# Row-wise attention scores: their causal mask from TensorE to VectorE and GpSimd

## The reference

```python
xn = layernorm(x)
q, k, v = (split_heads(xn @ W.T) for W in (Wq, Wk, Wv))
scores = einsum('bhqd,bhkd->bhqk', q, k) / sqrt(32)
scores = where(tril(ones((S, S))), scores, finfo.min)      # causal, S = 1024
attn = einsum('bhqk,bhkd->bhqd', softmax(scores), v)
gate = silu((xn @ fp8(gate_w)) * gate_scale)               # 512 -> 1536
up = (xn @ fp8(up_w)) * up_scale
ffn = ((gate * up) @ fp8(down_w)) * down_scale             # 1536 -> 512
out = x + merge_heads(attn) @ Wo.T + ffn
```

## Time and profile before

| | |
|---|---|
| median of 3 runs | 1274.52 us (1270.1 to 1280.29) |
| the profiled execution | 1273.23 us |
| its span, first to last instruction | 1271.4 us |
| mean granted TensorE clock | 0.993 |
| PE, DVE, ACT, POOL busy | 96%, 81%, 71%, 69% |

### The profile page before, as it was taken

How to read it: one execution, slowest core, us unless ns; L and a number is a source line. 1 busy time by engine, 2 the same in 40 slices (tenths; PEclk the granted TensorE clock), 3 DMA queues, 4 the chain that set the end, 5 groups by cost and what they waited for, 6 DMA issues and landing times.

```text
span 1271.4 us, 32677 instructions
## 1 busy us (share of the span) xinstructions
PE 1225.1 (96%) x11851; PEld 827.8 (65%) x11852; DVE 1031.0 (81%) x2587; ACT 908.6 (71%) x1555; POOL 875.1 (69%) x1033
## 2 busy tenths in 40 slices
PE   4999998979999999999999999999999999999988
PEld 3444443438677767677777777777777677777763
DVE  8877776768788888888888898888888888888862
ACT  4433433439788878887878898888888887878880
POOL 1333323227777777888888888888888888888882
PEclk9999999989999999999999999999999999999999
DMA  8799989776747485656667676757685766667555
GB/s 268 226 244 258 260 239 237 203 212 142 145 97 160 105 145 114 151 113 147 131 142 156 129 151 129 155 105 157 117 169 118 161 117 145 131 140 154 116 118 126
DMA packets 422319, 201.32 MB, mean 158 GB/s; under 512 B 327056, under 2 KB 390544, under 8 KB 421648
## 3 DMA queue, kind: packets, MB, share of 16 engines
q1 hardware_dynamic: 409312, 179.32, 64.1%
q10 hardware_dynamic: 12848, 19.93, 5.2%
HBM read 76.03 MB, written 44.30 MB: 95 GB/s over the span
## 4 chain that ended last, share of the span: by engine, by line
PE 65%; DMA 3%; ACT 3%; POOL 2%; issue 2%; DVE 2%; SPq 1%; ACTq 0%
PE bank L1653 22%; PE bank L1667 12%; PE bank L1631 10%; PE pair L241 5%; PE pair L1593 5%; PE bank L1675 4%; PE pair L1607 3%; PE pair L1675 2%; DMA p_t<-row 1%; POOL row L1338 1%; PE bank L1690 1%; DMA a_rows<-a_rows 1%; ACT probs L1390 1%; PE bank L294 1%; ACT row L1414 1%
## 5 line engine op out<-in xcount | busy, mean ns | idle before, releaser
L1400 ACT ACTIVATE p<-pair,s_exp 128x512 f32<-128x512 f32 (+1 forms) x384 | 243.5, 634 | 151.2 <-PE pair L1593 144.7
L1338 POOL TENSOR_TENSOR row<-row 128x896 f16<-128x896 f32 (+1 forms) x128 | 256.8, 2010 | 25.5 <-ACT row L1414 25.4
L1171 POOL TENSOR_TENSOR probs<-p,probs 128x512 f16<-128x512 f32 x192 | 221.1, 1158 | 6.8 <-ACT probs L1390 6.6
L1390 ACT CAST probs<-p 128x512 f16<-128x512 f32 (+1 forms) x384 | 215.1, 560 | 7.6 <-POOL p L1332 7.5
L1653 PE MATMUL bank<-shared,wg 128*128 128x256 f16 x1536 | 200.0, 273 | 0.7 <-DVE fu L1531 0.5
L1653 PE MATMUL bank<-shared,wu 128*128 128x256 f16 x1536 | 199.2, 273 | 0.0
L1667 PE MATMUL bank<-wd,fuse 128*128 128x512 f16 x768 | 193.1, 378 | 0.8 <-DVE ff_out L1517 0.8
L1332 POOL TENSOR_SCALAR_AFFINE_SELECT p<-p 128x128 f32<-128x128 f32 (+1 forms) x256 | 109.0, 428 | 103.0 <-ACT p L1400 100.8
L1536 DVE TENSOR_REDUCE row_top<-pair 128x1 f32<-128x896 f32 (+1 forms) x128 | 147.5, 1152 | 25.7 <-PE pair L1611 24.4
L1653 PEld LDWEIGHTS bank<-shared,wg 128*128 128x128 f16 x1536 | 144.3, 98 | 33.6 <-DMA shared<-xn_parts 1.3
L1653 PEld LDWEIGHTS bank<-shared,wu 128*128 128x128 f16 x1536 | 142.2, 98 | 19.5
(11 more groups left out here) (166 smaller groups left out, 2112.3 us busy)
## 6 DMA issues: line engine op xcount, KB each, us to landing
q_st<-q_parts SPq DMA_DIRECT2D x192, 64.0 KB, 2.3
k_st<-k_parts SPq DMA_DIRECT2D x192, 64.0 KB, 1.9
v_parts<-res SPq DMA_DIRECT2D x8, 1056.0 KB, 6.3
v_sb<-v_parts SPq DMA_DIRECT2D x64, 132.0 KB, 2.2
xn_parts<-x_t SPq DMA_DIRECT2D x16, 512.0 KB, 6.6
shared<-xn_parts SPq DMA_DIRECT2D x16, 512.0 KB, 4.7
res<-in_L_attn_x SPq DMA_DIRECT2D x16, 512.0 KB, 4.0
out<-shared SPq DMA_DIRECT2D x32, 256.0 KB, 2.5
```

The source lines that it names most:

```text
L1171: ops.tensor_tensor(probs[n % 2][:, LO, at], p32[e % RING][:, 0:UNIT_WIDTH[u]], probs[n % 2][:, HI, at], ALU.subtract).then_inc(signal, 1)
L1338: nc.gpsimd.tensor_tensor(row16[r][:, w:2 * w], row32[r][:, :], row16[r][:, 0:w], ALU.subtract).then_inc(row_lo, 1)
L1390: nc.scalar.copy(probs[n % 2][:, HI, u * 512:u * 512 + w], p32[e % RING][:, 0:w]).then_inc(p_hi, 1)
L1400: nc.scalar.activation(p32[e % RING][:, 0:w], st_bank[u % 2][:, 0:w], ACT.Exp, scale=s_exp[:, :]).then_inc(exp_done, 1)
```

## The change

The third product of a row tile goes, with its two bf16 tiles. DVE now takes the maximum over the columns ahead of the diagonal block, and then with a second instruction the maximum over the diagonal block plus the mask, starting from the first. The diagonal block's exponentials are therefore unmasked in `row32`, and POOL zeroes their masked half (`cut_row`). ACT's cast waits for POOL's select instead of the exponential. The casts move by one step (6 to 7, 12 to 13), and so do the low parts (8 to 9, 14 to 15).

```diff
--- before.py
+++ after.py
@@ -133,8 +133,9 @@
 ROW_SCORES_STEP = {2: (0,), 6: (1,)}
 ROW_MAX_STEP = {3: (0,), 6: (1,)}
 ROW_EXP_STEP = {4: (0,), 10: (1,)}
-ROW_HIGH_STEP = {6: (0,), 12: (1,)}
-ROW_LOW_STEP = {8: (0,), 14: (1,)}
+ROW_CUT_STEP = {4: (0,), 10: (1,)}
+ROW_HIGH_STEP = {7: (0,), 13: (1,)}
+ROW_LOW_STEP = {9: (0,), 15: (1,)}
 M_STEP = {8: (0, 1), 10: (2,), 11: (3,), 12: (4,), 14: (5,), 16: (6, 7)}
 MAX_STEP = {8: (0, 1), 10: (2,), 12: (3, 4), 13: (5,), 16: (6, 7)}
 MAX_HIGH_STEP = {1: (0,)}
@@ -1068,8 +1069,6 @@
         p_t = sb("p_t", [P, PT_SIZE], F16)
         row_top = sb("row_top", [P, 2], F32)
         row_bias = sb("row_bias", [P, 2], F32)
-        mask_bf = sb("mask_bf", [P, P], mybir.dt.bfloat16)
-        ident_bf = sb("ident_bf", [P, P], mybir.dt.bfloat16)
         rsum = sb("rsum", [P, QB // 2], F32)
         attn = sb("attn", [P, 2, QB, D], F32)
         a_rows = sb("a_rows", [P, 4 * D], F16)
@@ -1108,7 +1107,8 @@
         p_hi = sem("p_hi")
         p_lo_dve = sem("p_lo_dve")
         p_lo_pool = sem("p_lo_pool")
-        bf_set = sem("bf_set")
+        row_open = sem("row_open")
+        row_cut = sem("row_cut")
         row_mm = sem("row_mm")
         row_red = sem("row_red")
         row_bias_set = sem("row_bias_set")
@@ -1301,8 +1301,6 @@
             pool.sem_inc(res_done, 1)
             nc.gpsimd.memset(k_st[3][3 * DK:3 * DK + 2, :], MSCALE).then_inc(ones_set, 1)
             pool.wait_ge(ones_set, 1)
-            nc.gpsimd.tensor_copy(mask_bf[:, :], rows.mask[:, 512 - P:512]).then_inc(bf_set, 1)
-            nc.gpsimd.tensor_copy(ident_bf[:, :], ident[:, :]).then_inc(bf_set, 1)
 
             def add_down(i, t):
 
@@ -1332,6 +1330,13 @@
                 nc.gpsimd.affine_select(out=at, in_=at, compare_op=ALU.is_ge, fill=0.0, base=0,
                                         pattern=[[0, blocks], [1, P]], channel_multiplier=-1).then_inc(diag_done, 1)
 
+            def cut_row(r, n):
+
+                pool.wait_ge(row_exp, 2 * n + r + 1)
+                at = row32[r][:, row_width(r) - P:row_width(r)]
+                nc.gpsimd.affine_select(out=at, in_=at, compare_op=ALU.is_ge, fill=0.0, base=0, pattern=[[-1, P]],
+                                        channel_multiplier=1).then_inc(row_cut, 1)
+
             def low_of_row(r, n):
                 pool.wait_ge(row_hi, 2 * n + r + 1)
                 w = row_width(r)
@@ -1342,6 +1347,8 @@
                 n, k = HEADS_PER_IT * it + s, s * U + u
                 for unit, head in of_head(SELECT_STEP, n, u):
                     select(unit, head)
+                for r, head in of_head(ROW_CUT_STEP, n, u):
+                    cut_row(r, head)
                 for unit, head in of_head(LOW_POOL_STEP, n, u):
                     take_low(pool, nc.gpsimd, POOL_LOW, unit, head, p_lo_pool)
                 for r, head in of_head(ROW_LOW_STEP, n, u):
@@ -1408,7 +1415,7 @@
                                      bias=row_bias[:, r:r + 1], scale=s_exp[:, :]).then_inc(row_exp, 1)
 
             def high_of_row(r, n):
-                act.wait_ge(row_exp, 2 * n + r + 1)
+                act.wait_ge(row_cut, 2 * n + r + 1)
 
                 wait(act, row_turned[r], 16 * n)
                 nc.scalar.copy(row16[r][:, 0:row_width(r)], row32[r][:, :]).then_inc(row_hi, 1)
@@ -1533,8 +1540,12 @@
 
             def maximum_of_row(r, n):
                 dve.wait_ge(row_mm, 2 * n + r + 1)
-                nc.vector.tensor_reduce(row_top[:, r:r + 1], row_bank[r][:, 0:row_width(r)], AX.X, ALU.max
-                                        ).then_inc(row_red, 1)
+                w, top = row_width(r), row_top[:, r:r + 1]
+                nc.vector.tensor_reduce(top, row_bank[r][:, 0:w - P], AX.X, ALU.max).then_inc(row_open, 1)
+                dve.wait_ge(row_open, 2 * n + r + 1)
+                nc.vector.tensor_tensor_reduce(
+                    out=rows.junk[r][:, 0:P], in0=row_bank[r][:, w - P:w], in1=rows.mask[:, 512 - P:512], scale=1.0,
+                    scalar=top, op0=ALU.add, op1=ALU.max, accum_out=top).then_inc(row_red, 1)
                 dve.wait_ge(row_red, 2 * n + r + 1)
                 nc.vector.tensor_scalar(row_bias[:, r:r + 1], row_top[:, r:r + 1], s_neg[:, 0:1], None, ALU.mult
                                         ).then_inc(row_bias_set, 1)
@@ -1604,12 +1615,9 @@
                     pe.wait_ge(exp_done, NE * n + 3)
                 part, i, w = slice(0, 3 * DK), ROWS[r], row_width(r)
                 for at, size in ((0, 512), (512, w - 512)):
-                    nc.tensor.matmul(row_bank[r][:, at:at + size], q_st[s][part, i * P:(i + 1) * P],
-                                     k_st[s][part, at:at + size], start=True, stop=at == 0)
-                if n == r == 0:
-                    pe.wait_ge(bf_set, 2)
-                nc.tensor.matmul(row_bank[r][:, w - P:w], ident_bf[:, :], mask_bf[:, :], start=False,
-                                 stop=True).then_inc(row_mm, 1)
+                    mm = nc.tensor.matmul(row_bank[r][:, at:at + size], q_st[s][part, i * P:(i + 1) * P],
+                                          k_st[s][part, at:at + size], start=True, stop=True)
+                mm.then_inc(row_mm, 1)
 
             def probabilities(n, i, j, part):
 
```

## The result

The changed kernel took 1326.65 us, median of four runs (1324.98 to 1329.09), against 1276.12 us of the kernel before: 1.0407 times as long, 95% interval 1.0364 to 1.0449. Its profiled execution has a span of 1324.1 us at a mean granted clock of 0.991, against 1271.4 at 0.993; by an estimate from these, a clock lower by 0.2% is worth under 3 of the 52.7 us.

What follows compares the result with a forecast made beforehand. TensorE (PE, 96% busy) was taken to bound the kernel, with the cut making it wait for POOL's chain: 1273 + 42 (iterations 4 to 15) + 6 (iterations 0 to 3) = 1321 us, range 1284 to 1355.

Steps and rivals of the forecast that it cites:

- the likeliest case: POOL's late selects delay ACT's row-1 cast and stall PE at full size: from the cheap end to 1355 us, 55%.
- The chain: Row 1's select waits behind row 0's low part on POOL, delaying ACT's cast and tanh, DVE's fu, PE's gate.
- the three named: Heads s = 2, 3 and 1 of each four-head iteration: PE stalls 2.45 (2.0), 1.1 (0.6), 0.8 (0.6) us.
- the wrong wait: In head s = 1, PE stalls 0.8 (0.6) us at gate 5 through the late cast and its tanh.
- 3.8 us less 0.3 of gain per iteration: PE stalls of 3.8 us per four-head iteration, less product gain: 3.5 x 12 iterations (4 to 15) = 42 us.
- the cheap end: POOL's selects at 0.29 us instead of 0.40: stalls of 3.2 us per iteration instead of 4.35.
- the rule: VectorE and GpSimd lock each other out of shared SBUF ports; by it the new selects would be cheap throughout.
- 1312 us: Whole-kernel time with selects at the cheap end throughout: 1273 + 2.9 x 12 + 4, against 1330 at the dear end.
- At most 7.4 us: PE's gain from dropping 128 mask products at 0.058 us each, 0.6% of the time.
- cost nothing more: DVE's 0.45 us stalls at PE's third maxima unit, heads 2 and 3, lie ahead of larger stalls there.
- the rival: Only DVE bites: PE's third maxima unit waits, +0.45 in heads 2 and 3, +0.2 in head 1; 1284 us, 12%.
- The hidden-work rival: POOL's and ACT's waits are absorbed and TensorE's 7.4 us come through: 1266 us, 10%.

Runs made afterwards that it cites:

- pool_only: The changed kernel with the mask products kept on PE and DVE's single maximum kept, so POOL's selects and the casts' waits stand alone: 1327.66 us, 1.0444.
- cut1_early: The changed kernel with row 1's select issued in step 9 instead of 10, ahead of row 0's low part in POOL's list: 1295.88 us, 1.0191.
- pe_dve_only: The changed kernel without POOL's selects, steps as before: no mask products, maximum in two steps, masked half of the exponentials left unzeroed: 1281.36 us, 1.0077.
- no_mask: The kernel before without the 128 mask products and nothing in their place, masked half of the row-wise scores left as it is: 1269.7 us, 0.9986.
- one_pass: The kernel before without mask products; one DVE instruction adds a wide mask in place in PSUM and takes the row maximum, no selects: 1271.87 us, 1.0002.
- placed: The whole change, row 0's select behind m_neg and m_part, row 1's ahead of row 0's low part only where s = 2, low parts at old steps: 1288.6 us, 1.0134.

## Why the prediction was right

The time (1321 us forecast, 1326.65 measured) is inside the range, and it is the likeliest case, not a rival, that happened. By its own steps:

*The chain.* Select behind row 0's low part, cast of row 1, tanh, `fu`, PE's gate: each link is in the waits, and `pool_only` shows that POOL's part is enough by itself. The longer heads are the three named, and head s = 0 has no stall. For s = 2 and s = 3 `cut1_early` shows the chain, as they get 1.34 and 0.71 us shorter when the select comes early. For s = 1 it shows that the prediction had the wrong wait: its 0.96 us stay when the stall at gate 5 goes, and come from POOL's own lateness by ACT's cast of `probs`. It is luck that 0.96 is near the 0.8 (0.6) of the forecast.

*Its size.* 3.8 us less 0.3 of gain per iteration was forecast, 3.82 measured; for the iterations without `a_rows` 1.5, measured 1.8. By head the forecast of the stalls was 2.45 (2.0), 1.1 (0.6) and 0.8 (0.6) us for s = 2, 3 and 1; the heads are 1.80, 1.17 and 0.96 longer, products' gain included. The cast in s = 2 is 2.6 us late, which is the cheap end (2.65). So the choice of 3.8 between the ends came out for a partly wrong reason: the selects are at the cheap end throughout,

```profile
L1337 POOL TENSOR_SCALAR_AFFINE_SELECT row<-row x128: 283/292/311, 282.3 to 1279.6; 128x128 f32<-128x128 f32 x128
```

as the rule had it that the prediction cites from "SBUF — State Buffer" of the Trainium skill, while the time that I worked out from that, 1312 us, was 15 short. The prices of s = 3 and s = 1 are larger than the cheap end gave. The idle times ahead of the cast, 1.98, 1.25 and 0.87 us in s = 2, 3 and 1, are shorter than the 2.5 to 3, 2 and 1 to 1.5 announced, because ACT itself comes later to the cast: in s = 2 it had waited 0.41 us for PE's scores ahead of the exponential before it, and waits 0.91 now.

*PE's gain.* "At most 7.4 us" holds as a bound, and is far too high as a value: 2 us. In the sum this hid, since it counted only 0.3 us an iteration; the changed kernel has 0.19 (63.25 us against 63.44 in `pool_only`). The 0.06 us per product is its time on one chain; without the products, an iteration of the kernel before is 0.31 us shorter instead of 0.46, and the whole run gains less still.

*DVE.* That its stalls "cost nothing more" is right for the changed kernel: it takes no longer than `pool_only`. The timelines of PE in head 34 show how, the changed kernel first:

```profile
815.14 0.34 PE L242 MATMUL pair<-k_st,q_st 96*128 96x384 f16 x1 [0.42 <-DVE mx L265]
...
823.54 1.05 PE L1661 MATMUL bank<-shared,wg 128*128 128x256 f16 x8 [1.17 <-DVE fu L1538]
...
824.42 1.05 PE L1664 MATMUL bank<-shared,wg 128*128 128x256 f16 x8 [1.39 <-DVE fu L1542]
```

PE waits 0.42 us at the third maxima unit, where `pool_only` doesn't wait, and less from there to gate 9, which it starts in step with `pool_only` (12.12 and 12.13 us after row 0's exponential). In head s = 3 the same happens ahead of the next head's first scores, where PE waits 2.8 us in all for ACT instead of 9.5: the idle time that the prediction announced there has mostly moved to the maxima. But alone these stalls cost: `pe_dve_only` is at 1281.36 us where the rival said 1284, with 0.5 us in each of the heads 2 and 3 where it said 0.45, and nothing in head 1 where it said 0.2. Its 12 us above `no_mask` go with 0.25 us of DVE work per row tile, and `one_pass`, with 0.07 per tile, is about 2 above it. This is what a repair of POOL's order runs into (`placed`), beside the selects' own work in s = 1; no place that was tried makes the change pay.

*The hidden-work rival* asked for less than 0.6 us of delay of the cast. It was refuted twice: the delay is 2.6 us, and with nothing delayed at all the gain is 2 us, not 7.

No version here is faster than the kernel before by more than the 0.14% of `no_mask`, whose row-wise scores go unmasked; `one_pass`, which masks them all, equals it.

## What to carry to other kernels

Work that is taken off the busiest engine is worth what the engine gains before its next wait, not its time in the array: leave it out altogether in a trial before finding it a new home (here 2 us, where its new home cost 52). When work moves to a queue that runs in written order, walk that queue to the instruction in front of it; moving one 0.29 us select per head ahead of a 1.9 us instruction was worth 31 us. Then look for the stretch in which that queue has no gap: there added work is paid for wherever it stands (here 0.5 us in each head s = 1). If a sum is masked anyway on an engine that reads the data, write it back in the same pass rather than masking again elsewhere.

## What the runs showed of the hardware

- A DVE instruction on two SBUF tiles (128x512, 0.68 us alone) stretched to as much as 2.66 us beside POOL's SBUF instructions; in the two places looked at it ended 0.55 and 0.54 us after POOL's end. Its recorded time includes the block, so a long mean of such a line can be another engine's work.
- The same holds the other way round. A select of 128x128 on POOL took 283 to 311 ns in all 128 places of the changed kernel, while selects of exponentials reach 862. In the kernel before, 13 selects of 128x128 and 13 of 128x256 (of 220 that its timelines show one by one) were stretched, to 0.74 to 0.75 and 0.85 to 0.86 us. Each of them ended 0.14 to 0.16 and 0.26 to 0.27 us after a DVE low part, an instruction on two SBUF tiles, such as these, POOL first:

```profile
651.52 0.74 POOL L1332 TENSOR_SCALAR_AFFINE_SELECT p<-p 128x128 f32<-128x128 f32 x1
...
651.29 0.82 DVE L1171 TENSOR_TENSOR probs<-p,probs 128x512 f16<-128x512 f32 x1
```

  None of the new selects overlaps such an instruction, and they are at the cheap end.

- A masked maximum over 1024 columns that writes them back to PSUM takes 1225 ns on average, the plain maximum 1217; the accumulator's read adds 0.14 us when the output is in PSUM and 0.08 when it is in SBUF.
